# A 128-row form of the bias products in the two fp6 linear layers of a macaron block

## The reference, cut to what matters

```python
x = x + 0.5 * _L1_ffn_ref(_layernorm(x, axis=-1), L1_ffn_weight, L1_ffn_bias)
x = x + _L1_attn_ref(_layernorm(x, axis=-1), ...)
x = x + 0.5 * _L1_ffn_ref(_layernorm(x, axis=-1), L1_ffn_weight, L1_ffn_bias)
```

## Time and profile before

| | |
|---|---|
| median of 3 runs | 2545.14 us (2542.69 to 2546.99) |
| the profiled execution's own time | 2547.16 us |
| its span, first to last instruction | 2545.1 us |
| share of the span: PE, PE's weight loads, DVE, ACT, POOL | 84%, 64%, 60%, 38%, 12% |
| first linear layer | about 1426 to 1642 us |
| final linear layer | about 2414 us to the end |
| mean granted TensorE clock | 0.91 of full speed |

### The profile page before, as it was taken

One profiled execution on the slowest core, in us unless ns is written; L12 is line 12 of the kernel. 1 busy time (PEld: TensorE's weight loads), 2 busy tenths in 40 slices (PEclk: granted clock), 3 DMA queues, 4 the chain that ended last, 5 costly groups with the idle time before them and its releaser, 6 DMA issues.

```text
span 2545.1 us, 38488 instructions
## 1 busy us (share of the span) xinstructions
PE 2141.1 (84%) x13354; PEld 1631.8 (64%) x13354; DVE 1514.6 (60%) x3516; ACT 978.4 (38%) x1961; POOL 313.3 (12%) x284
## 2 busy tenths in 40 slices
PE   4589999967899956899999456589999999999857
PEld 2478888856788935788888335445555555555445
DVE  7744434347455576434343588676876776777286
ACT  4222323222333342232323244236555656555532
POOL 4320000031000044100000432311002002000000
PEclk8799999978999987999999766689999999999955
DMA  8120110111000041101100220433423423412001
GB/s 261 41 66 24 31 30 26 30 60 31 1 1 1 1 116 56 52 28 30 31 27 28 79 58 25 65 55 59 51 28 70 58 27 70 58 27 28 9 17 50
DMA packets 84031, 114.82 MB, mean 45 GB/s; under 512 B 12213, under 2 KB 73817, under 8 KB 80729
## 3 DMA queue, kind: packets, MB, share of 16 engines
q1 hardware_dynamic: 77416, 94.80, 17.2%
q0 software_dynamic: 6432, 17.57, 2.2%
HBM read 69.16 MB, written 43.17 MB: 44 GB/s over the span
## 4 chain that ended last, share of the span: by engine, by line
PE 72%; DVE 18%; ACT 4%; issue 2%; DMA 2%; POOL 1%; ACTq 0%; DVEq 0%; SPq 0%; POOLq 0%
PE psum L775 10%; PE psum L777 10%; PE psum L776 10%; PE psum L2287 5%; PE psum L2266 5%; PE psum L126 5%; PE psum L2240 5%; PE psum L128 4%; PE psum L127 4%; PE psum L2270 3%; PE psum L862 3%; PE psum L2244 2%; DVE stats L160 2%; DVE m L2163 2%; DVE xn L185 1%
## 5 line engine op out<-in xcount | busy, mean ns | idle before, releaser
L2125 ACT ACTIVATE pt<-psum 128x512 f32<-128x512 f32 (+3 forms) x768 | 343.7, 491 | 265.1 <-DVE psum L2193 159.0
L2163 DVE TENSOR_REDUCE m<-psum 128x1 f32<-128x512 f32 (+2 forms) x576 | 379.2, 687 | 81.9 <-PE psum L2244 43.2
L740 DVE SCALAR_TENSOR_TENSOR h<-psum,xg,sg 128x128 f32<-128x128 f32 x592 | 166.7, 344 | 415.4 <-PE psum L862 415.4
L556 ACT ACTIVATE sg<-psum 128x512 f32<-128x512 f32 x180 | 107.5, 597 | 575.0 <-PE psum L777 575.0
L775 PE MATMUL psum<-w_hi,xt_hi 128*128 (+1 forms) x720 | 285.5, 396 | 34.6 <-DVE xt_lo L705 34.6
L776 PE MATMUL psum<-w_lo,xt_hi 128*128 (+1 forms) x720 | 283.9, 394 | 0.0
L777 PE MATMUL psum<-w_hi,xt_lo 128*128 (+1 forms) x720 | 283.5, 394 | 0.0
L2240 PE MATMUL psum<-ks,qs 96*128 96x512 bf16 (+3 forms) x768 | 245.3, 338 | 17.4 <-DMA ks<-qk_scr 9.2
L2266 PE MATMUL psum<-qs,ks 99*128 99x512 bf16 (+3 forms) x768 | 242.8, 332 | 20.0 <-ACT pt L2125 14.2
L775 PE MATMUL psum<-w_hi,ht_hi 128*128 (+1 forms) x720 | 218.4, 303 | 0.2
L2270 PE MATMUL psum<-band,ident_r 128*128 128x256 f32 (+1 forms) x864 | 216.4, 338 | 0.0
(11 more groups left out here) (284 smaller groups left out, 4278.3 us busy)
## 6 DMA issues: line engine op xcount, KB each, us to landing
xg<-w_dram SPq DMA_DIRECT2D x54, 256.0 KB, 3.2
qk_scr<-parts SPq DMA_DIRECT2D x32, 384.0 KB, 2.5
qs<-qk_scr SPq DMA_DIRECT2D x96, 128.0 KB, 7.2
ks<-qk_scr SPq DMA_DIRECT2D x96, 128.0 KB, 7.9
xg<-rows_in SPq DMA_DIRECT2D x74, 132.0 KB, 2.2
rows_out<-yb SPq DMA_DIRECT2D x74, 128.0 KB, 1.7
x<-x_dram SPq DMA_DIRECT2D x4, 1024.0 KB, 8.8
out_dram<-x SPq DMA_DIRECT2D x4, 1024.0 KB, 4.4
```

Of the source, the lines that this page charges most:

```text
L556: act.activation(sg[i % 2][:, :, :], up_banks(i)[:, :, 0:F], ACT.Silu).then_inc(*silu.up())
L740: ins = dve.scalar_tensor_tensor(out=h[i % 2][:, e, :], in0=u[:, e, :], scalar=xg[j % XSLOT][:, at:at + 1], in1=sg[i % 2][:, e, :], op0=AL ...
L2125: act.activation(pt[n % NPT][:, 0:q1 - q0], st_bank(n)[:, 0:q1 - q0], ACT.Exp).then_inc(*exped.up())
L2163: dve.tensor_reduce(m3[:, h, at:at + (n - 1) * step + 1:step], mx_ring.bank((kind, i)).rearrange("p (n k) -> p n k", k=wide), AXIS.X, ALU. ...
```

## The change: what it does

The tiles of the bias product are made 128 rows high: `bias`, `bias_hi`, `bias_2`, `low_row`, `minus` and `ones`. POOL fills the whole of `bias` with zeros before the two DMAs write rows 0 and 1, and SP waits for that before it issues them. The other 126 rows stay zero in `bias_2` and -1 in `ones`.

```diff
-                bias, bias_hi, bias_2 = sb(st, "bias", [2, D]), sb(st, "bias_hi", [2, D], F32R), sb(st, "bias_2", [2, D], F32R)
-                low_row, minus, ones = sb(st, "low_row", [2, 1]), sb(st, "minus", [2, P]), sb(st, "ones", [2, P], F32R)
+                bias, bias_hi, bias_2 = sb(st, "bias", [P, D]), sb(st, "bias_hi", [P, D], F32R), sb(st, "bias_2", [P, D], F32R)
+                low_row, minus, ones = sb(st, "low_row", [P, 1]), sb(st, "minus", [P, P]), sb(st, "ones", [P, P], F32R)
...
+                    sp.wait_ge(*S("ones")(1))
                     for row in range(2):
                         sp.dma_start(bias[row:row + 1, :], fb_d.unsqueeze(0)).then_inc(*S.dma("w_in1").up())
...
                     pool.memset(low_row[:, :], 1.0)
+                    pool.memset(bias[:, :], 0.0)
                     pool.memset(minus[:, :], -1.0).then_inc(*S("ones").up())
                     pool.wait_ge(*S("ones")(1))
                     pool.memset(low_row[0:1, :], 0.0).then_inc(*S("ones").up())
```

## The result

The changed kernel takes 2522.52 us (median of 4 runs, 2519.18 to 2522.83), the kernel before 2543.91 us in the same comparison (4 runs, 2538.3 to 2546.99). The ratio is 0.9916, with a 95% interval of 0.9899 to 0.9933: 21 us faster. In a second comparison it was 2518.58 us (4 runs) against 2543.25 us (9 runs), a ratio of 0.9897 (0.9880 to 0.9913). The profiled execution took 2522.7 us with a span of 2520.6 us, 24.5 us less than the span before.

What follows compares the result with a forecast made beforehand. In the final layer DVE and PE were taken to bound the kernel in a loop. 12.9 + 4.3 + 6.6 - 0.3 - 0.65 = 22.9 us from pauses plus 4.1 us clock, 27.0 us off the median: 2518.1 us, range 2513 to 2528 us.

Steps and rivals of the forecast that it cites:

- The pauses come from the row count: Bias products in both linear layers: 128 rows save 0.59 us a group at half clock, 0.39 us at full.
- The rival that rows don't matter: Pause belongs to the change of operands or a group's start in PSUM; only the head's loss left, 2546.1 us; chance 0.09.
- the half-way one: Pause ahead of the bias product stays, the one behind it goes: near 2534 us; chance 0.08.
- Six steady quads, 12.9 us: Final layer: DVE's `sum` stops waiting for PE in six quads, period near 11.9 us, 12.9 us saved.
- The tail, 4.3 us and 3.7 us: Final layer's last two quads: 4.3 us from the pauses, 3.7 us from the clock rising to full.
- The head, -0.65 us and -0.3 us: Final layer: later bias DMA issue costs 0.65 us; first layer: POOL's larger memset costs 0.3 us.
- The first layer, 6.6 us less 0.3 us, and 0.4 us for the clock: Four places with PE on the path give 6.6 us, memset costs 0.3 us, clock gives 0.4 us in the last burst.
- The second place: First layer, the `sum` at 1539.76 waiting 0.57 us for PE: 0.6 us saved.
- the third place: First layer, ACT waiting for PE until 1619.75 behind four bias products at the full clock: 1.6 us saved.
- my slower rival: Pauses stay and the first layer's warm stretch behind 1613.60 is lost: 4.6 us, with the head 5.6 us, 2550.8 us; chance 0.03.
- the likeliest case: Whole kernel: pauses go and the clock rises as forecast, 2518.1 us, own range 2514 to 2522 us; chance 0.60.
- the rival whose clock stays at half: The pauses go but the tail's clock stays at half: 2522.2 us; chance 0.20.

Runs made afterwards that it cites:

- PE kept busy: The kernel before, two-row bias products, plus overwritten 128-row products ahead of PE's wait for `xt_lo` in the final layer: 2535.62 us (6 runs), ratio 0.9962.
- the late bias: The changed kernel with the final layer's bias copies moved behind the first `centre` and `bias_2` ahead of the first `less`: 2517.17 us, ratio 0.9893; again 2517.99 us.

## Why the prediction was right, point by point

*The pauses come from the row count.* Right, and now shown: with all else of the change in place and two rows used, nothing is gained, and the pauses go between 64 and 65 rows. The rival that rows don't matter, and the half-way one, are out. The sizes were right to a hundredth: 1.50 us a group for 1.49 us at the half clock, 0.83 us for 0.82 us at the full one.

*Six steady quads, 12.9 us.* 12.86 us measured, with a loss of 0.80 us at the head in it, so 13.7 us. The period is 11.71 us and not 11.9 us, since both `sum` instructions now run back to back: 1.28 us for the two, where they took 3.60 us with the wait. DVE took over as the limit, with 58.9 us of work in 60 us.

*The tail, 4.3 us and 3.7 us.* 8.80 us measured. Six runs with 128 rows there gave 10.02 to 10.67 us, the four with two rows 11.8 (PE kept busy), 13.6, 14.05 and 18.83 us. What the prediction had wrong is the reason for the clock's share. It took the half clock of the last burst before for a consequence of the pauses. But a two-row burst ran at the full clock in the run that used two rows, and in others. The profile of before had a slow tail, 5 us longer than two of the others, so that a part of the 8.8 us is the luck of the execution that was read. With the change the full clock came every time: all six had it in the last burst, three of them with a seventh burst mostly at half. How much of the 8.8 us an average execution gains, the runs don't settle.

*The head, -0.65 us and -0.3 us.* -0.80 us in the final layer (1.89 to 2.69 us), of which 0.60 us is the later issue, as forecast, and 0.19 us the DMA's longer way to `bias_hi`. That second part is chance: the five other runs with this head have `centred` at 2.40 to 2.54 us. POOL's memset took 0.32 us for the 0.31 us of the nearest row. The loss can be had back: with the late bias `centred` starts at 0.75 us. In the first layer the memset cost 0.22 us for 0.3 us: DVE's first `sum` is 3.04 us later than before (1508.91 for 1505.87), POOL's first memset 2.82 us.

*The first layer, 6.6 us less 0.3 us, and 0.4 us for the clock.* The mis-sized term: 4.52 us came for 6.7 us. Followed by the same instructions, the profile of after is 2.82 us late at the start and 0.85 us late at the first projection's wait (1571.17 for 1570.32): 1.97 us gained for 2.5 us forecast. The `sum` at 1523.70 gave more than its 2.2 us, since both now take 1.28 us for 3.60 us: 2.32 us. But 0.80 us of that was lost at once, in DVE's `last_bit`. Before, and then with the change:

```profile
1527.58 0.69 DVE L1471 TENSOR_SCALAR centred<-centred 128x1024 uint32<-128x1024 uint32 x1
```

```profile
1527.97 1.26 POOL L1667 TENSOR_TENSOR band<-band_full,band 128x512 fp32r<-128x512 f32 x1 [13.17 <-ACT band L1688]
1528.29 1.49 DVE L1473 TENSOR_SCALAR centred<-centred 128x1024 uint32<-128x1024 uint32 x1
```

Before, POOL's `band` also started at 1527.97, behind `last_bit`. So it is in all twelve traces: in the six in which DVE comes to it 0.2 to 0.3 us behind POOL's start, `last_bit` takes 1.49 to 1.58 us, in the six in which it starts ahead of POOL, 0.69 us. This is a collision that the forecast didn't look for. The second place gave 0.65 us for 0.6 us. The wait of 0.50 us at 1558.13, costed at nothing, did turn into a wait for ACT, 1.76 us ahead of an `amax` where it was 1.17 us.

At the third place, worth 1.6 us in the sum, 0.49 us came (1621.16 for 1620.80). The clock rose some 2.2 us later into the same piece of work and stood at 0.50 from 1613.60 to 1616.70, so that the missing pauses were partly paid back. This is the mechanism of my slower rival, with 1.1 us of its 4.6 us. Another 0.35 us was lost at the next projection (1628.14 for 1627.43), where ACT waited longer for a DMA. But the trace of before was a lucky one at the third place: DVE's wait there is 4.96, 5.65, 8.57, 8.62 and 8.68 us in the five traces with two rows, and 4.08 to 4.76 us in the six with over 64 rows. The last burst gave 2.41 us for the 2.6 us.

*The sum.* 27.0 us were forecast and 21.4 us measured in the first comparison, 24.7 us in the second; between the two profiles it was 24.5 us, of which 26.2 us in the two linear layers. The rest, -2.8 us ahead of them and 1.1 us in the attention, is what executions differ by. Most of what is missing between 24.5 and 21.4 us comes from taking gains that were read in an execution of 2547.16 us off a median 2 us below it, 3.25 us below it in the comparison. So 2522.52 us lies within the range, but 0.5 us outside the narrower one of the likeliest case, and right on the 2522.2 us of the rival whose clock stays at half. That is a coincidence: the last burst ran at 1.00, and the time comes from the short gain of the first layer, the later start and that difference of executions.

## What to carry to other kernels

Look at the steps between products of the same shape in a burst, and for products with few rows among full ones: here one with up to 64 rows cost 0.59 us more at the half clock, and zeros up to 65 rows or more made it cost only its columns. What such a pause is worth depends on who waits behind the burst: with 2.2 us of DVE's idle time in a period, 2.3 us could be had and no more. An engine that is set free earlier may run into another: look at what it then starts beside. And where a gain rests on the granted clock of one profile, look at several executions before putting a number to it.

## What the runs showed of the hardware that I had not expected

The pauses are a step between 64 and 65 rows, and a product of 33 rows is as slow as one of 2. Moments of rise and fall of TensorE's clock shift from one execution to the next and with small changes of timing, and with it the tail of the two-row kernels lay anywhere between 13.6 and 18.8 us (11.8 us with PE kept busy). The kernel before spread over 2538.3 to 2548.8 us in the comparisons, the changed one over 2516.6 to 2522.8 us. The clock goes with that spread: of 22 executions of the kernel before, the seven under 2543 us have a mean granted clock of 0.910 to 0.915, the six over 2546 us one of 0.906 to 0.909. That it makes most of the spread isn't shown by that.

DVE's `last_bit` took 1.49 to 1.58 us for 0.69 us wherever it started behind POOL's `band` and beside it.
